# A test-time memory with its buffers zeroed by GpSimd, and a feed-forward whose weights arrive in three groups

## What is computed

```python
xn = _layernorm(x)
x = x + _L0_attn_ref(xn, ...) + _L0_ffn_ref(xn, ...)
xn = _layernorm(x)
x = x + _L1_attn_ref(xn, ...) + _L1_ffn_ref(xn, ...)
...
```

```python
xn = (x - mu) / sqrt(var + 1e-05) * g + bln
a, gate = split(xn @ W1 + b1)
return a * gelu(gate) @ W2 + b2
```

## Time and profile before

| | |
|---|---|
| median of 3 runs | 4624.53 us |
| lowest, highest | 4623.03, 4631.54 us |
| the profiled execution, its own time | 4631.24 us |
| its span, first to last instruction | 4629.2 us |
| mean granted TensorE clock | 0.918 |
| PE busy | 3973.7 us (86%) |
| DVE busy | 3218.2 us (70%) |
| ACT busy | 2538.6 us (55%) |
| POOL busy | 1194.1 us (26%) |
| chain that ended last | PE 64%, DVE 14%, issue 9%, ACT 8%, DMA 2%, SPq 2% |

### The profile page before, as it was taken

The page is one execution under the profiler, slowest core; times in us unless marked ns, Lnnn a source line. Parts: engine busy times, 40 slices in busy tenths (PEclk is TensorE's granted clock), DMA queues, the critical chain, the costliest instruction groups (busy, mean ns, idle before and its releaser), DMA issues.

```text
span 4629.2 us, 114349 instructions
## 1 busy us (share of the span) xinstructions
PE 3973.7 (86%) x46974; PEld 2224.8 (48%) x46974; DVE 3218.2 (70%) x5216; ACT 2538.6 (55%) x3730; POOL 1194.1 (26%) x1015
## 2 busy tenths in 40 slices
PE   3688888888888888867768999999997599999997
PEld 1355555555555555535544555555554233333333
DVE  7688888888889888946533666666664676767772
ACT  4356666656566566643222555555553266666665
POOL 0265555555556555500000000000000011111110
PEclk6899999999999999975567999999998699999999
DMA  0122222222222222210100000000000301000000
GB/s 17 66 57 71 66 62 71 66 62 76 61 72 66 59 74 66 62 28 17 24 11 16 3 3 2 3 4 4 3 1 10 111 13 24 18 18 18 18 1 14
DMA packets 84464, 166.55 MB, mean 36 GB/s; under 512 B 22472, under 2 KB 36472, under 8 KB 82704
## 3 DMA queue, kind: packets, MB, share of 16 engines
q1 hardware_dynamic: 83952, 159.13, 13.2%
HBM read 40.60 MB, written 8.52 MB: 11 GB/s over the span
## 4 chain that ended last, share of the span: by engine, by line
PE 64%; DVE 14%; issue 9%; ACT 8%; DMA 2%; SPq 2%; POOL 1%; DVEq 0%; ACTq 0%; POOLq 0%
PE banks L503 6%; PE banks L1238 5%; PE banks L2171 5%; PE banks L1221 4%; PE banks L1209 4%; PE banks L582 4%; PE banks L598 3%; PE banks L544 3%; PE banks L618 2%; PE banks L561 2%; ACT arena L2309 2%; PE banks L2145 2%; PE banks L535 2%; ACT arena L710 2%; PE banks L2129 2%
## 5 line engine op out<-in xcount | busy, mean ns | idle before, releaser
L2383 DVE TENSOR_REDUCE arena<-banks 128x2 f32<-128x1024 f32 x512 | 614.3, 1223 | 277.8 <-PE banks L2136 145.4
L2309 ACT ACTIVATE arena<-banks 128x1024 f32<-128x1024 f32 x512 | 522.5, 1025 | 280.9 <-PE banks L2152 147.2
L939 POOL TENSOR_TENSOR arena<-arena 128x512 f32<-128x512 f32 x384 | 425.4, 1130 | 757.7 <-DVE arena L824 750.2
L943 POOL TENSOR_TENSOR arena<-arena 128x1024 f32<-128x1024 f32 x192 | 533.1, 2777 | 15.0
L1391 DVE CUSTOM_DVE_ANT_0 arena<-arena,banks 128x512 f32<-128x512 f32 (+3 forms) x640 | 361.8, 603 | 233.7 <-issue 232.4
L1334 ACT ACTIVATE arena<-banks 128x512 f32<-128x512 f32 (+3 forms) x320 | 170.1, 532 | 409.4 <-PE banks L1221 408.7
L503 PE MATMUL banks<-arena 128*128 128x512 f32 x768 | 355.4, 606 | 31.1 <-ACT arena L673 24.2
L2171 PE MATMUL banks<-arena 128*32 128x256 f32 x4096 | 335.9, 395 | 13.0 <-issue 7.8
L1326 ACT ACTIVATE arena<-arena 128x128 f32<-128x128 f32 (+15 forms) x256 | 328.5, 1285 | 11.9 <-DVE arena L1403 6.7
L1209 PE MATMUL banks<-arena 64*128 64x512 f32 (+3 forms) x1280 | 322.9, 582 | 5.0 <-issue 3.8
L1221 PEld LDWEIGHTS banks<-consts,arena 128*128 128x128 f32 x2176 | 233.1, 141 | 187.9 <-DVE arena L1410 101.9
(11 more groups left out here) (431 smaller groups left out, 7630.0 us busy)
## 6 DMA issues: line engine op xcount, KB each, us to landing
arena<-arena SPq DMA_DIRECT2D x768, 64.0 KB
arena<-arena SPq DMA_DIRECT2D x96, 384.0 KB, 3.6
arena<-arena SPq DMA_DIRECT2D x96, 128.0 KB, 3.4
arena<-in_lf_wqkv SPq DMA_DIRECT2D x6, 1024.0 KB, 5.2
arena<-features_k SPq DMA_DIRECT2D x32, 128.0 KB
arena<-arena SPq DMA_DIRECT2D x8, 512.0 KB
arena<-features_q SPq DMA_DIRECT2D x16, 216.0 KB
arena<-in_lf_wqkv SPq DMA_DIRECT2D x6, 512.0 KB, 3.8
```

The lines of the kernel that those rows point to most:

```text
L939: nc.gpsimd.tensor_tensor(r[:, :, e * H2:(e + 1) * H2], q[:, j, :, (1 - e) * H2:(2 - e) * H2], s[:, j, 1, e * H2:(e + 1) * H2].unsqueeze(1 ...
L943: nc.gpsimd.tensor_tensor(a, a, lf_rb, ALU.add).then_inc(S("lf_rot" + x), 1)
L2309: nc.scalar.activation(bi_PT[n % 4], PS[:, 2 * bi_slot("S", n):2 * bi_slot("S", n) + 2].rearrange("p a b -> p (a b)"), ACT.Exp).then_inc(S ...
L2383: nc.vector.tensor_reduce(bi_max[j % 2][:, t, :, c], PS[:, 2 * slot:2 * slot + 2], AX.X, ALU.max).then_inc(S("bi_mx"), 1)
```

## The change

In the six-layer branch the one group of loads becomes three. `lf_load_up` brings W1 and the norm's gain and bias (semaphore lf_w1_in), `lf_load_gate` the six columns of b1 (lf_b1_in), and `lf_load_down` W2 with b2 as its 385th column (lf_w2_in): four DMAs instead of three. All stand in step s = 24 ahead of the eight copies: the first behind a wait for the last `up` of the layer and ahead of `shift_v`, the second behind `shift_v` and the last `product`, the third behind lf_y. `normed` on DVE waits for no weights any more, and gain and bias are applied by ACT (`affine`), at j = 1 between `squares` and `keep_q`.

In the memory branch GpSimd zeroes tt_gp and tt_rp, ACT copies the projections ahead of the gates, and the root with its reciprocal becomes a logarithm and an exponential on ACT.

```diff
@@ -357,9 +357,10 @@
...
         lf_w1 = arena.f32(2 * FF)
-        lf_w2 = arena.f32_3(3, P)
+        lf_w2b = arena.f32(3 * P + 1)
+        lf_w2 = lf_w2b[:, 0:3 * P].rearrange("p (a b) -> p a b", a=3)
         lf_qsk = arena.f32(4 * DH)
-        lf_vec = arena.f32(9)
+        lf_vec = arena.f32(8)
@@ -427,10 +428,15 @@
         def lf_load_wo(sp, l):
...

-        def lf_load_ffn(sp, l):
-            sp.dma_start(lf_w1, d["lf_w1"][l].rearrange("o p f -> (o p) f")).then_inc(S("lf_wf_in"), 16)
-            sp.dma_start(lf_w2, d["lf_w2"][l].rearrange("o p a b -> (o p) a b")).then_inc(S("lf_wf_in"), 16)
-            sp.dma_start(lf_vec, d["lf_vec"][l].rearrange("o p f -> (o p) f")).then_inc(S("lf_wf_in"), 16)
+        def lf_load_up(sp, l):
+            sp.dma_start(lf_w1, d["lf_w1"][l].rearrange("o p f -> (o p) f")).then_inc(S("lf_w1_in"), 16)
+            sp.dma_start(lf_vec[:, 0:2], d["lf_vec"][l].rearrange("o p f -> (o p) f")[:, 0:2]).then_inc(S("lf_w1_in"), 16)
+        def lf_load_gate(sp, l):
+            sp.dma_start(lf_vec[:, 2:8], d["lf_vec"][l].rearrange("o p f -> (o p) f")[:, 2:8]).then_inc(S("lf_b1_in"), 16)
+        def lf_load_down(sp, l):
+            sp.dma_start(lf_w2b, d["lf_w2"][l].rearrange("o p f -> (o p) f")).then_inc(S("lf_w2_in"), 16)
...
         def lf_sp(sp):
@@ -440,7 +446,9 @@
...
             lf_load_wo(sp, first)
-            lf_load_ffn(sp, first)
+            lf_load_up(sp, first)
+            lf_load_gate(sp, first)
+            lf_load_down(sp, first)
...
             def shift_v(n, l):
@@ -473,16 +481,22 @@
...
                     lf_load_v(sp, following)
+                if more and s == NB + 8:
+                    sp.wait_ge(S("lf_amm"), l * 12 + 12)
+                    lf_load_up(sp, following)
...
                     shift_v(s - 1, l)
+                if more and s == NB + 8:
+                    sp.wait_ge(S("lf_h"), l * 12 + 12)
+                    lf_load_gate(sp, following)
+                    sp.wait_ge(S("lf_y"), l * NCH + 2 * NCH)
+                    lf_load_down(sp, following)
...
                     lf_load_wo(sp, following)
-                if more and s == NB + 8:
-                    sp.wait_ge(S("lf_y"), l * NCH + 2 * NCH)
-                    lf_load_ffn(sp, following)
@@ -612,13 +626,15 @@
...
                     if c % NCH == 0:
-                        pe.wait_ge(S("lf_wf_in"), (l + c // NCH) * 48 + 48)
+                        pe.wait_ge(S("lf_w1_in"), (l + c // NCH) * 32 + 32)
...
             def down(c, l):
                 pe.wait_ge(S("lf_h"), l * 12 + (3 * c + 3))
+                if c % NCH == 0:
+                    pe.wait_ge(S("lf_w2_in"), (l + c // NCH) * 16 + 16)
@@ -741,15 +757,21 @@
...

+            def affine(c, l):
+                act.wait_ge(S("lf_xhat"), l * NCH + (c + 1))
+                if c % NCH == 0:
+                    act.wait_ge(S("lf_w1_in"), (l + c // NCH) * 32 + 32)
+                nc.scalar.activation(lf_xc, lf_xc, ACT.Identity, scale=lf_vec[:, 0:1], bias=lf_vec[:, 1:2]).then_inc(S("lf_xf"), 1)
             def gate(c, m, l):
...
                 if m == 0 and c % NCH == 0:
-                    act.wait_ge(S("lf_wf_in"), (l + c // NCH) * 48 + 48)
+                    act.wait_ge(S("lf_b1_in"), (l + c // NCH) * 16 + 16)
...
                 act.wait_ge(S("lf_gmm"), l * 12 + (3 * c + m + 1))
-                nc.scalar.activation(lf_G[m][0:k], PS[0:k, 6], ACT.Gelu, bias=lf_vec[0:k, 6 + m:7 + m]).then_inc(S("lf_gelu"), 1)
+                nc.scalar.activation(lf_G[m][0:k], PS[0:k, 6], ACT.Gelu, bias=lf_vec[0:k, 5 + m:6 + m]).then_inc(S("lf_gelu"), 1)
...
             def step(l, s, end):
@@ -759,6 +781,8 @@
...
                     nc.scalar.preload_act_table_set(LN_EXP_SET)
+                if ffn and j == 1:
+                    affine(c, l)
@@ -859,23 +883,23 @@
...
             def normed(c, l):
                 dve.wait_ge(S("lf_dev"), l * NCH + (c + 1))
-                if c % NCH == 0:
-                    dve.wait_ge(S("lf_wf_in"), (l + c // NCH) * 48 + 48)
                 nc.vector.tensor_tensor(lf_xc, lf_xc, lf_sx, ALU.mult).then_inc(S("lf_xhat"), 1)
-                dve.wait_ge(S("lf_xhat"), l * NCH + (c + 1))
-                nc.vector.tensor_scalar(lf_xc, lf_xc, lf_vec[:, 0:1], lf_vec[:, 1:2], ALU.mult, ALU.add).then_inc(S("lf_xf"), 1)
...
             def product(c, m, l):
...
                 dve.wait_ge(S("lf_gelu"), l * 12 + (3 * c + m + 1))
+                if m == 0 and c % NCH == 0:
+                    dve.wait_ge(S("lf_b1_in"), (l + c // NCH) * 16 + 16)
                 dve.wait_ge(S("lf_amm"), l * 12 + (3 * c + m + 1))
-                nc.vector.scalar_tensor_tensor(out=lf_G[m][0:k], in0=PS[0:k, 7], scalar=lf_vec[0:k, 3 + m:4 + m], in1=lf_G[m][0:k],
+                nc.vector.scalar_tensor_tensor(out=lf_G[m][0:k], in0=PS[0:k, 7], scalar=lf_vec[0:k, 2 + m:3 + m], in1=lf_G[m][0:k],
...
             def out_(c, l):
...
                 dve.wait_ge(S("lf_o"), l * NCH + (c + 1))
-                nc.vector.scalar_tensor_tensor(out=ck(lf_y[:, 1:T + 1], f), in0=PS[:, 7], scalar=lf_vec[:, 2:3], in1=ck(lf_y2[:, 1:T + 1], f),
+                if c % NCH == 0:
+                    dve.wait_ge(S("lf_w2_in"), (l + c // NCH) * 16 + 16)
+                nc.vector.scalar_tensor_tensor(out=ck(lf_y[:, 1:T + 1], f), in0=PS[:, 7], scalar=lf_w2b[:, 3 * P:3 * P + 1], in1=ck(lf_y2[:, 1:T + 1], f),
...
             def step(l, s, end):
@@ -1728,14 +1752,13 @@
...
             for c in range(NCH):
+                act.wait_ge(S("tt_kvq"), c + 1)
+                nc.scalar.activation(ck(tt_xp[:, 3:T + 3], c)[0:96], PS[0:96, c], ACT.Copy).then_inc(S("tt_xp"), 1)
+            for c in range(NCH):
...
                 nc.scalar.activation(ck(tt_th, c)[hi], PS[hi, 4 + c], ACT.Identity, bias=gb[hi]).then_inc(S("tt_sig"), 1)
-            for c in range(NCH):
-                act.wait_ge(S("tt_kvq"), c + 1)
-                nc.scalar.activation(ck(tt_xp[:, 3:T + 3], c)[0:96], PS[0:96, c], ACT.Copy).then_inc(S("tt_xp"), 1)
@@ -1756,6 +1779,7 @@
...
             nc.scalar.activation(tt_gp[lo, :, G_v:G_v + 64], chunks(tt_c, slice(32, 64)), ACT.Copy, scale=2.0)
+            act.wait_ge(S("tt_zero"), 2)
@@ -1806,17 +1830,16 @@
...
                 act.wait_ge(S("tt_oms"), c + 1)
-                nc.scalar.activation(ck(tt_ors, c), PS[:, c], ACT.Sqrt, bias=tt_eps[:, 0:1]).then_inc(S("tt_ostd"), 1)
+                nc.scalar.activation(ck(tt_ors, c), PS[:, c], ACT.Ln, bias=tt_eps[:, 0:1]).then_inc(S("tt_oln"), 1)
+                act.wait_ge(S("tt_oln"), c + 1)
+                nc.scalar.activation(ck(tt_ors, c), ck(tt_ors, c), ACT.Exp, scale=-0.5).then_inc(S("tt_ostd"), 1)
...
         def tt_dve(dve):
...
             nc.vector.memset(tt_eps, 1e-6).then_inc(S("tt_eps"), 1)
-            st(nc.vector.memset(tt_mhalf, -0.5))
-            st(nc.vector.memset(tt_rp[32:64], 0.0))
-            st(nc.vector.memset(tt_gp[0:64], 0.0))
-            nc.vector.memset(tt_wn, 0.0).then_inc(S("tt_zero"), 1)
-            dve.wait_ge(S("tt_zero"), 1)
+            nc.vector.memset(tt_wn, 0.0).then_inc(S("tt_wn0"), 1)
+            dve.wait_ge(S("tt_wn0"), 1)
@@ -1845,6 +1868,7 @@
...

+            dve.wait_ge(S("tt_zero"), 2)
@@ -1937,12 +1961,16 @@
...
                 dve.wait_ge(S("tt_ostd"), c + 1)
-                st(nc.vector.reciprocal(ck(tt_ors, c), ck(tt_ors, c)))
...
         def tt_pool(pool):
+            nc.gpsimd.memset(tt_mhalf, -0.5).then_inc(S("tt_half"), 1)
+            pool.wait_ge(S("tt_half"), 1)
+            nc.gpsimd.memset(tt_gp[0:64], 0.0).then_inc(S("tt_zero"), 1)
             pool.wait_ge(S("tt_zero"), 1)
+            nc.gpsimd.memset(tt_rp[32:64], 0.0).then_inc(S("tt_zero"), 1)
+            pool.wait_ge(S("tt_zero"), 2)
...
             def grad(n, p, pair, ret):
@@ -2578,11 +2606,11 @@
...
     w2[:, :FF] = f["L0_ffn_W2"]
-    o["lf_w2"] = w2.reshape(D, 3, P, P).transpose(0, 2, 1, 3)
+    o["lf_w2"] = np.concatenate([w2.reshape(D, 3, P, P).transpose(0, 2, 1, 3).reshape(D, P, 3 * P), f["L0_ffn_b2"][:, :, None]], 2)
...
     b1 = b1.reshape(2, D, 3, P).transpose(0, 2, 1, 3).reshape(6, D, P)
-    o["lf_vec"] = np.concatenate([np.stack([f["L0_ffn_ln_g"], f["L0_ffn_ln_b"], f["L0_ffn_b2"]]), b1]).transpose(1, 2, 0)
+    o["lf_vec"] = np.concatenate([np.stack([f["L0_ffn_ln_g"], f["L0_ffn_ln_b"]]), b1]).transpose(1, 2, 0)
```

## The result

| | before | after |
|---|---|---|
| median, lowest, highest (4 runs each, same chip) | 4628.03, 4623.03, 4634.24 us | 4572.61, 4570.23, 4581.28 us |
| ratio, 95% interval | | 0.9883, 0.9864 to 0.9902 |
| the profiled execution, its span | 4631.24, 4629.2 us | 4570.23, 4568.1 us |
| granted TensorE clock | 0.918 | 0.926 |
| PE, DVE, ACT, POOL busy | 3973.7, 3218.2, 2538.6, 1194.1 us | 3949.6, 3199.0, 2570.1, 1209.2 us |

The medians are 55.4 us apart, the predicted sum was 56.7. The 95% interval of the ratio is a gain of 45 to 63 us. The predicted total, 4568, stood on a median of 4624.5 of three runs; with the fourth run the kernel before has 4628.0, which is 3.5 of the 4.6 us between 4568 and 4572.6.

A forecast was written before the change was run, and what follows sets the result against it. DVE's waits for late feed-forward loads lengthen five steps, and DVE is last in the short ones too; terms 37.2 + 9.6 + 2.4 + 6.2 + 1.3 = 56.7 us off the median 4624.5 give 4568, range 4553 to 4588.

The forecast's parts named there:

- Part 1: Six-layer branch, weights in groups: DVE's wait for feed-forward loads goes whole, five long steps become like the others, 37.2 us.
- Part 2: Six-layer branch, gain and bias moved from DVE to ACT: 0.45 us in each of 22 steps, 9.6 us net.
- its end moves too, by 0.2 to 0.5: Steps j = 1: GpSimd's instruction, with which DVE's clamp ends, would itself end 0.2 to 0.5 us earlier.
- The signs: Expected in the trace: steps j = 1 at 17.3 to 17.6 us, PE's wait before L549 at 0.6 to 0.8.
- Rival (d): The tail or the move of gain and bias gives nothing: total 4574 to 4578; chance 0.10.
- rival (a): Steps j = 1: DVE's removed operation comes through whole, 1.15 instead of 0.45 us, 15 us more: 4553; chance 0.10.
- Part 3: Memory branch's start: projection copies run ahead of the gates, so PE's L1677 starts earlier, 2.4 us; memsets' going gives nothing.
- Part 4: Memory branch's tail: reciprocals replaced by logarithm and exponential on ACT, 6.2 us, plus a table load saved before L1546, 1.3.
- Rival (b): Memory branch's tail: one table set serves logarithm and exponential, ACT no longer bounds it, 6.9 us less: 4561; chance 0.07.
- (c): Layer passes: first weight group lands late or another wait takes over; half the weights' gain goes, 4587, or all, 4605; chance 0.08.
- (e): Slower: `affine` in ACT's queue ahead of `keep_q` waits for DVE, which waits for GpSimd; total 4645; chance 0.02.
- (f): The change doesn't do what it says: a semaphore still couples the groups, only the memory branch's gains remain: 4615; chance 0.02.

The follow-up runs named there:

- one_group_early: The kernel before, with its single group of three feed-forward loads issued ahead of the eight copies instead of behind them; median 4590.0 us, ratio 0.990 to 0.994.
- affine_on_dve: The changed kernel with gain and bias applied by DVE again instead of ACT; median 4579.6 us, ratio 0.9874 to 0.9912.
- tail_one_set: The changed kernel with the table set holding both logarithm and exponential asked for once before the tail's loop; median 4571.3 us, ratio 0.9856 to 0.9890.
- copies_after_gates: The changed kernel with the four copies of the projections put behind the sigmoids and biases of the gates again; one run, 4578.2 us.
- memsets_on_dve: The changed kernel with the three buffers of the memory branch zeroed by DVE again instead of GpSimd; one run, 4577.6 us.
- clamp_in_log: The changed kernel without DVE's clamp of the squared norms, the lower bound added as the logarithm's bias instead; median 4521.1 us, ratio 0.9745 to 0.9785.

## Why the prediction was right, and where its terms were off

**Part 1, 37.2 us: right.** The five long steps became like the others, and the trace gives 37.9 with their share of part 2 in it (7.42 to 7.84 each). The three groups were issued where the prediction put them, the first 0.3 us behind the issue of the last copy of step 23, before `shift_v`. one_group_early shows the cause: the place, not the split.

**Part 2, 9.6 us: the right mechanism, the size off.** I took 0.45 us a step between the bounds 0 and 1.15, "since the end of L943 is the nearer row". The end of GpSimd's instruction did decide, but it moved by 0.17, not by 0.2 to 0.5: GpSimd's two L963 take 2.52 us now, where the two L939 took 2.69 in the same step before; L866's share of their slowing went, and that is the 0.17. So 0.18 us a step, 3.7 us in 21 steps by affine_on_dve, against 9.6. The step of the prediction that failed is "its end moves too, by 0.2 to 0.5", and with it the 0.45 us a step. The signs say the same: steps j = 1 at 17.73 and 17.76 instead of 17.3 to 17.6, and PE's wait before L549 at 1.09 instead of 0.6 to 0.8. Rival (d), which gave part 2 nothing, came nearer than the 9.6, and rival (a) is out. `affine` itself took 0.81 us, not 0.69, under cover.

**Part 3, 2.4 us: right.** L1677 came 2.7 us sooner behind the first issue, all from the order of the copies; the memsets were hidden, as costed.

**Part 4, 6.2 + 1.3 us: right.** The tail gave 22.1 - 15.99 = 6.1, the missing load 1.3. Rival (b) was excluded by the earlier trace rows and the trace bears that out: eight loads of 1.28 us. The prediction wrote of rows 8 that the next instruction follows at once. It does not there: the next exponential starts at 69.37, 4.65 us behind the load's end, waiting for DVE, so that place could not show what a load costs behind itself. The tail can: the exponential starts at 2304.56, 0.01 us behind the end of its load. Of the two rules of the Trainium skill that the prediction weighed, one load for a logarithm with an exponential (ScalarE: Activation LUTs, Table sets: the hidden batching unit) was seen only where the kernel asks for the set that has both, as tail_one_set does. The other, 2.66 us for a switch with its drain (the Trainium skill, ScalarE: Activation LUTs, What ACT_TABLE_LOAD costs), was not seen: a load took 1.28 us with nothing behind it, and two activations and two loads fill the period of 3.94 us.

**The sum: right in part by luck.** The terms as the traces show them give 37.9 + 2.8 (16 plain steps) + 2.7 + 6.1 + 1.3 = 50.8 us, 5.9 less than forecast, nearly all of it in part 2. At L1546 the changed execution is 54.7 ahead. The rest of the six-layer branch makes most of the difference: the changed one is 1.5 us ahead at the first transposition, its steps of other kinds differ by up to 2.2 us either way, in sum 4.1 in its favour, and the end of the branch, after the last transposition, is 2.7 us longer (51.4 against 48.7), of which 1.65 is the last L632, 3.60 us instead of 1.95, with a granted clock of 0.53 over its length where it was 1.00:

```profile
1989.26 3.60 PE L632 MATMUL banks<-arena 128*85 128x512 f32 x4 [0.91 <-DVE arena L894]
```

This does not repeat. tail_one_set, copies_after_gates and memsets_on_dve have the same six-layer branch. From the first to the last transposition it took 1739.9, 1732.5 and 1740.0 us in them, where it took 1730.6 in the changed kernel's execution, and the last L632 took 1.95 us in all three. So the gain beyond the 50.8 us is no more than executions differ by, and that the total came so near to 56.7 is luck; both lie in the interval of 45 to 63. Rivals (c), (e) and (f) are excluded by the rows of the pass: no wait for in_lf_vec, and ACT's L711 waits for PE.

What the prediction missed was the larger thing beside it. It saw that L809 ends with GpSimd's instruction and used that as a bound on part 2. It did not ask what the hold itself was worth: with the change the clamp grew to 2 us in steps j = 1, and it was on the path, as clamp_in_log shows.

## What to carry to other kernels

Where a load is late, look first at what stands ahead of it in its queue; moving it gave 37 us here, splitting it nothing. Where an instruction's end coincides again and again with another engine's end, suspect that it is held, though the profile books it as busy and not as waiting, as it did with this clamp: compare its duration with that of the same shape where the other engine is idle, and try another form, or fold it away, before moving work off the engine in front of it. Where a logarithm and an exponential alternate, ask for the set that has both; here that took 6.8 us off the tail in the trace.

## What the runs showed of the hardware that was not expected

A clamp of 32 columns, 0.18 us alone, took 2.03 us beside a GpSimd instruction of 2.35 as a TENSOR_SCALAR, 2.08 as a TENSOR_TENSOR with two inputs, and 0.22 as a TENSOR_REDUCE.

A memset by GpSimd, which reads nothing, held a TENSOR_SCALAR too. DVE's L1847, in the changed kernel and in copies_after_gates:

```profile
2028.86 2.40 DVE L1847 TENSOR_SCALAR arena<-arena 96x2048 f32<-96x2048 f32 x1 [14.33 <-ACT arena L1756]
```

```profile
2038.45 1.34 DVE L1847 TENSOR_SCALAR arena<-arena 96x2048 f32<-96x2048 f32 x1 [23.04 <-ACT arena L1761]
```

In the first, GpSimd's memset of 12288 columns ended 1.32 us into it; in the second it ran alone. In the traces of the eight other kernels in which the two overlap, it took 2.30 to 3.05 us, and in all nine it ended 1.08 to 1.10 us behind the memset's end, wherever it had started. GpSimd fills 12288 columns of 32 partitions in 10.34 us, DVE in 10.30.
